# Attention scores in 64x64 products, exponentials head by head on ScalarE, and a new plan for the end of the experts

## The reference

```
chunks = x in 16 chunks of 64 tokens; Xh = rfft(chunks)          # 33 frequencies
A_low  = attention over the 4 lowest frequencies of all chunks (real and imaginary parts apart):
         16 heads of 64, 4 key/value heads, 64 positions, block-causal mask,
         p = softmax(q k^T / 8), o = p v, then the output weights
A_high = gelu(causal conv of width 7) @ weights, times a gate, plus X_high
x = layernorm(x + irfft([alpha*A_low + (1-alpha)*X_low, A_high]))
top 2 of 8 experts by distance, softmax weights;  expert: (silu(x Wg + bg) * (x W1 + b1)) W2 + b2, hidden 342
x = layernorm(x + sum of the two experts' outputs, weighted)
```

## Time and profile before

| | us |
|---|---|
| median of three runs | 608.26 |
| profiled execution | 609.42 |
| its span, first to last instruction | 607.6 |
| PE / DVE / ACT / POOL busy | 525.6 / 388.7 / 350.7 / 286.1 |
| granted TensorE clock, mean | 0.925 of full |

### The profile page before, as it was taken

How to read it: one execution, slowest core, us unless ns; L and a number is a source line. 1 busy time by engine, 2 the same in 40 slices (tenths; PEclk the granted TensorE clock), 3 DMA queues, 4 the chain that set the end, 5 groups by cost and what they waited for, 6 DMA issues and landing times.

```text
span 607.6 us, 13326 instructions
## 1 busy us (share of the span) xinstructions
PE 525.6 (87%) x3849; PEld 497.2 (82%) x3849; DVE 388.7 (64%) x1109; ACT 350.7 (58%) x738; POOL 286.1 (47%) x415
## 2 busy tenths in 40 slices
PE   3878999999999750086999999999999999999990
PEld 3767998988988530075999999999999999999990
DVE  3468899888899888991433345545464646466563
ACT  3456888887888412034555555575757565656751
POOL 0132544543544200605544444466776777563654
PEclk9979999997999955567999999999999999999995
DMA  8241055146152110111000000011111111000000
GB/s 232 61 120 55 15 149 161 43 120 161 30 131 71 35 35 2 12 13 29 19 20 20 15 20 21 20 29 33 37 38 37 33 32 37 28 29 10 32 32 35
DMA packets 48974, 31.14 MB, mean 51 GB/s; under 512 B 14251, under 2 KB 46582, under 8 KB 48918
## 3 DMA queue, kind: packets, MB, share of 16 engines
q1 hardware_dynamic: 43974, 20.87, 13.5%
q0 software_dynamic: 4224, 8.75, 5.2%
q10 hardware_dynamic: 720, 0.82, 0.5%
HBM read 21.73 MB, written 8.69 MB: 50 GB/s over the span
## 4 chain that ended last, share of the span: by engine, by line
PE 51%; POOL 3%; issue 3%; DVE 2%; DMA 1%; ACT 0%; POOLq 0%; DVEq 0%
PE ps L1434 25%; PE ps L1452 17%; PE ps L1442 8%; POOL out_dram L1401 1%; PE ps L1465 1%; DMA bias_parts<-blo 0%; POOL wo L1276 0%; DMA xs<-rows_dram,idx 0%; POOL we L1278 0%; POOL blo L1283 0%; POOL xs L1296 0%; POOL bhi L1281 0%; DVE Lc L1065 0%; POOL we L1275 0%; POOL wts L1290 0%
## 5 line engine op out<-in xcount | busy, mean ns | idle before, releaser
L1434 PE MATMUL ps<-wts,xh 128*128 x624 | 155.7, 333 | 1.0 <-issue 1.0
L1606 DVE TENSOR_TENSOR h<-ps,sg 128x684 f32<-128x684 f32 x78 | 67.9, 871 | 113.3 <-PE ps L1434 113.3
L1452 PE MATMUL ps<-w2s,hT 115*128 (+1 forms) x936 | 117.5, 275 | 1.0 <-DVE xs L1617 1.0
L1412 POOL TENSOR_TENSOR xl<-xT,xh 127x128 fp32r<-127x128 f32 x156 | 68.3, 459 | 102.1 <-ACT xh L1509 97.1
L1452 PEld LDWEIGHTS ps<-w2s,hT 115*128 115x128 f32 (+1 forms) x936 | 110.7, 191 | 1.4 <-issue 1.4
L1434 PEld LDWEIGHTS ps<-wts,xh 128*128 128x128 f32 x624 | 105.9, 192 | 1.4 <-issue 1.3
L1434 PE MATMUL ps<-wts,xl 128*128 x312 | 100.4, 322 | 0.0
L1520 ACT ACTIVATE sg<-ps 128x684 f32<-128x684 f32 x78 | 57.9, 742 | 68.6 <-PE ps L1434 68.3
L1528 ACT ACTIVATE hT<-ps 114x768 f32<-114x768 f32 x78 | 63.2, 810 | 56.9 <-PE ps L1442 56.0
L1617 DVE SCALAR_TENSOR_TENSOR xs<-ps,xs 128x128 f32 x156 | 54.3, 348 | 36.2 <-PE ps L1452 30.5
L1401 POOL DMA_INDIRECT out_dram<-xs,idx x64 | 63.0, 984 | 24.4 <-issue 18.1
(11 more groups left out here) (281 smaller groups left out, 878.9 us busy)
## 6 DMA issues: line engine op xcount, KB each, us to landing
xt<-_attn_hidden_states_dram SPq DMA_DIRECT2D x8, 512.0 KB, 6.0
xres<-_attn_hidden_states_dram SPq DMA_DIRECT2D x7, 512.0 KB, 5.3
rows_dram<-x1s SPq DMA_DIRECT2D x7, 512.0 KB, 3.7
w2s<-in_L_ffn_W_dram SPq DMA_DIRECT2D x8, 171.0 KB
st<-in_L_ffn_Wg_dram SPq DMA_DIRECT2D x8, 171.0 KB, 3.1
st<-in_L_ffn_W_dram SPq DMA_DIRECT2D x8, 171.0 KB, 3.6
stl<-in_L_ffn_Wg_dram SPq DMA_DIRECT2D x8, 171.0 KB, 3.5
stl<-in_L_ffn_W_dram SPq DMA_DIRECT2D x8, 171.0 KB, 4.1
```

The lines of the kernel that those rows point to most:

```text
L1412: v.tensor_tensor(xl[0:D - 1, i % 2, u, :], xT[0:D - 1, bass.ds(off[u], P)], xh[0:D - 1, i % 2, u, :].bitcast(F32), ALU.subtract).then_inc ...
L1434: mm = pe.matmul(ps[:, 2 * w + u, 0:HF], a[:, t % 2, u, :], wflat[:, bass.ds(w1[u] + (b + w * HF), HF)], start=(k == 0), stop=(k == 2))
L1452: mm = pe.matmul(ps[:, 6 + u, 0:D], hT[0:n, t % 2, u, k, :], w2flat[0:n, bass.ds(w1[2 + u] + k * D, D)], start=(k == 0), stop=(k == 2))
L1606: v.tensor_tensor(h[:, t % 2, :, :], ps[:, 2:4, 0:HF], sg[:, :, :], ALU.mult).then_inc(s["h_done"], 1)
```

## The change

Phase 1, scores. `QB` holds the queries without zeros, scaled by 1/8 in the eviction (two instructions a step in place of four). Each pair of heads is multiplied as two products of 64x64 weights, one with partitions 0 to 63 into PSUM partitions 0 to 63, one with 64 to 127. DVE takes only the maximum, negated. ACT takes the exponential slice by slice, straight from PSUM, with the negated maximum as bias, and writes the sum of the slice with `accum_out`. The subtraction and the sum on DVE go.

Phase 1, POOL. The three instructions for the squared norm move behind the next step's weight subtraction.

Phase 2. The last iteration runs its one real unit and writes its down product to other banks, so that it doesn't wait for the accumulation before it; the groups of tiles are smaller from tile 40 on; DVE issues up to nine pieces of normalisation an iteration, and after the last iterations 3 x 3; ACT and POOL take the iterations from a simulation of that plan (`norm_steps`).

```diff
-        QB = sb("QB", [P, 2, NHP, 2, LT])
+        QB = sb("QB", [P, 2, NHP, LT])
...
-            v.memset(QB[:, :, :, :, :], 0.0).then_inc(s["prep_cst"], 1)
...
                         for n in range(NHP):
-                            mm = pe.matmul(ps[:, 4 + i, n * LT:(n + 1) * LT], QB[:, i, n, :, :].rearrange("p a t -> p (a t)"),
-                                           kT[:, n // 2, i, :], start=False, stop=(n == NHP - 1))
+                            for h in range(2):
+                                q0 = h * HD
+                                mm = pe.matmul(ps[q0:q0 + HD, 4 + i, n * LT:(n + 1) * LT], QB[q0:q0 + HD, i, n, :],
+                                               kT[q0:q0 + HD, n // 2, i, :], start=False, stop=(n == NHP - 1))
...
-                        for h in range(2):
-                            q0 = h * HD
-                            nc.scalar.activation(QB[q0:q0 + HD, :, 4 * r:4 * r + 4, h, :]...,
-                                                 ps[q0:q0 + HD, 4 + r, :]..., ACT.Copy).then_inc(s["q_ev"], 1)
+                        nc.scalar.activation(QB[:, :, 4 * r:4 * r + 4, :].rearrange("p i n t -> p n i t"),
+                                                 ps[:, 4 + r, :]..., ACT.Copy, scale=1.0 / 8).then_inc(s["q_ev"], 1)
...
                 def softmax(i):
-                    act.wait_ge(s["sub_done"], 2 * t + i + 1)
-                    nc.scalar.activation(Sb[:, i, :, :], Sb[:, i, :, :], ACT.Exp, scale=1.0 / 8).then_inc(s["exp_done"], 1)
+                    act.wait_ge(s["max_done"], 2 * t + i + 1)
+                    if Y:
+                        act.wait_ge(s["pn_done"], 2 * t)
+                    for n in range(NHP):
+                        ins = nc.scalar.activation(Sb[:, i, n, :], ps[:, 4 + i, n * LT:(n + 1) * LT], ACT.Exp, bias=mx[:, i, n:n + 1],
+                                                   accum_out=sm[:, i, n:n + 1])
+                    ins.then_inc(s["exp_done"], 1)
...
-                    v.tensor_reduce(mx[:, i, :], sc, AX, ALU.max).then_inc(s["max_done"], 1)
-                    dve.wait_ge(s["max_done"], 2 * t + i + 1)
                     if Y:
-                        dve.wait_ge(s["pn_done"], 2 * t)
-                    v.tensor_tensor(Sb[:, i, :, :], sc, mx[:, i, :].unsqueeze(2).broadcast_to((P, NHP, LT)), ALU.subtract).then_inc(s["sub_done"], 1)
+                        dve.wait_ge(s["exp_done"], 2 * t)
+                    v.tensor_reduce(mx[:, i, :], sc, AX, ALU.max, negate=True).then_inc(s["max_done"], 1)
...
                         dve.wait_ge(s["exp_done"], 2 * t + i + 1)
-                        v.tensor_reduce(sm[:, i, :], Sb[:, i, :, :], AX, ALU.add).then_inc(s["sum_done"], 1)
-                        dve.wait_ge(s["sum_done"], 2 * t + i + 1)
                         v.reciprocal(rs[:, i, :], sm[:, i, :]).then_inc(s["rec_done"], 1)
...
             def step(t, X, Y, T):                 # POOL
                     v.tensor_tensor(st[:, 0:2 * HF], st[:, 0:2 * HF], stl[:, :], ALU.subtract).then_inc(s["wsub_done"], 1)
+                    if T:
+                        squares(t - 1)
...
-        n = 8 if k < NT - 16 else 4 if k < NT - 4 else 2
+        n = 8 if k < NT - 24 else 4 if k < NT - 4 else 2
...
+        def units(t):
+            return min(2, UNITS - 2 * t)
+        def low(t):
+            return 6 if t < ITER - 1 else 2
...
             def down(t, w1):
-                if t:
+                if 0 < t < ITER - 1:
                     pe.wait_ge(s["acc_done"], 2 * t)
-                for u in range(2):
+                for u in range(units(t)):
...
+            def norm(t, accumulated):
+                for _ in range(NORMS):
+                    if norm_due(groups, at, t, accumulated):
+                        at[:] = [at[0] + 1, 0] if piece(*at) else [at[0], at[1] + 1]
...
+def norm_due(groups, at, t, accumulated):
+    b, j = at
+    if b == len(groups):
+        return False
+    k0, n = groups[b]
+    return j >= n or t >= k0 + j + SETTLE + (2 if accumulated else 3)
...
+def norm_steps(groups):
+    out, at = [], [0, 0]
+    for t in range(ITER + 2):
+        for accumulated in (False,) * (2 * NORMS if t < ITER else 0) + (True,) * (NORMS if t < ITER else 3 * NORMS):
+            if norm_due(groups, at, t, accumulated):
+                at[1] += 1
+                if at[1] == groups[at[0]][1] + 14:
+                    out.append(t)
+                    at[:] = [at[0] + 1, 0]
+    return out + [ITER + 2] * (len(groups) - len(out))
```

More of the change, by code:

```diff
@@ L31 @@
 WE = 4 * HF
+NORMS = 3
 GATS = 4
@@ L942, in _, with squares @@
             pool.wait_ge(s["c15_done"], 1)
+            def squares(t):
+                pool.wait_ge(s["rstd_done"], t)
+                v.tensor_tensor(ya[:, :], y0[:, :], y0[:, :], ALU.mult).then_inc(s["newton"], 1)
+                v.tensor_tensor(yb[:, :], mv[:, :, 1], c128[:, :], ALU.mult).then_inc(s["newton"], 1)
+                pool.wait_ge(s["newton"], 8 * t)
+                v.tensor_tensor(sq[:, bass.ds((t - 1) * TB, TB)], ya[:, :], yb[:, :], ALU.mult).then_inc(s["sq_done"], 1)
             def step(t, X, Y, T):
@@ L1409, in _ @@
                         pool.wait_ge(s["prep"], 3)
-                    for u in range(2):
+                    for u in range(units(i)):
                         pool.wait_ge(s["xh_done"], 2 * i + u + 1)
@@ L1416, in _ @@
                 for n in range(1 if t + GAHEAD < NT else 2):
-                    if sent < NT and normed_by(groups, group_of, sent, DONE) < t:
+                    if sent < NT and out_by[group_of[sent]] + 1 < t:
                         scatter(sent)
@@ L1445, in down @@
             def down(t, w1):
-                if t:
+                if 0 < t < ITER - 1:
                     pe.wait_ge(s["acc_done"], 2 * t)
-                for u in range(2):
+                for u in range(units(t)):
                     for k in range(3):
                         n = HG + 1 if k == 0 else HG
-                        mm = pe.matmul(ps[:, 6 + u, 0:D], hT[0:n, t % 2, u, k, :],
+                        mm = pe.matmul(ps[:, low(t) + u, 0:D], hT[0:n, t % 2, u, k, :],
                                        w2flat[0:n, bass.ds(w1[2 + u] + k * D, D)], start=(k == 0), stop=(k == 2))
@@ L1507, in _ @@
                         act.wait_ge(s["a_done"], i - 1)
-                    for u in range(2):
+                    for u in range(units(i)):
                         nc.scalar.activation(xh[0:D - 1, i % 2, u, :], xT[0:D - 1, bass.ds(off[u], P)], ACT.Copy).then_inc(s["xh_done"], 1)
                 n = 0
-                while sent < NT and n < 2 and normed_by(groups, group_of, sent, DONE) <= t:
+                while t < ITER - 1 and sent < NT and n < 2 and out_by[group_of[sent]] + 2 <= t:
                     normed(sent)
@@ L1519, in _ @@
                         act.wait_ge(s["h_done"], t)
-                    nc.scalar.activation(sg[:, :, :], ps[:, 0:2, 0:HF], ACT.Silu).then_inc(s["sg_done"], 1)
+                    nc.scalar.activation(sg[:, 0:units(t), :], ps[:, 0:units(t), 0:HF], ACT.Silu).then_inc(s["sg_done"], 1)
                 if k < NT:
@@ L1527, in _ @@
                     act.wait_ge(s["b_done"], b + 1)
-                    nc.scalar.activation(hT[0:HG, b % 2, :, :, :].rearrange("p u k m -> p u (k m)"), ps[0:HG, 4:6, 0:3 * P],
+                    n = units(b)
+                    nc.scalar.activation(hT[0:HG, b % 2, 0:n, :, :].rearrange("p u k m -> p u (k m)"), ps[0:HG, 4:4 + n, 0:3 * P],
                                          ACT.Copy).then_inc(s["hT_done"], 1)
+                n = 0
+                while t >= ITER - 1 and sent < NT and n < 2 and out_by[group_of[sent]] <= t:
+                    normed(sent)
+                    sent += 1
+                    n += 1
             for k in range(sent, NT):
@@ L1588, in _ @@
             at = [0, 0]
-            def norm(t):
-                b, j = at
-                if b == len(groups):
-                    return
-                k0, n = groups[b]
-                if j < n and t < k0 + j + DONE:
-                    return
-                at[:] = [b + 1, 0] if piece(b, j) else [b, j + 1]
+            def norm(t, accumulated):
+                for _ in range(NORMS):
+                    if norm_due(groups, at, t, accumulated):
+                        at[:] = [at[0] + 1, 0] if piece(*at) else [at[0], at[1] + 1]
             for t in range(LAST + 1):
@@ L1605, in _ @@
                     dve.wait_ge(s["a_done"], t + 1)
-                    v.tensor_tensor(h[:, t % 2, :, :], ps[:, 2:4, 0:HF], sg[:, :, :], ALU.mult).then_inc(s["h_done"], 1)
+                    v.tensor_tensor(h[:, t % 2, 0:units(t), :], ps[:, 2:2 + units(t), 0:HF], sg[:, 0:units(t), :], ALU.mult).then_inc(s["h_done"], 1)
                 if c >= 0:
                     off = offsets(mybir.EngineType.DVE, c, 2, [RTOP] * 2 + [RTOP + D + E] * 2)
-                norm(t)
-                norm(t)
+                if t < ITER:
```

(21 more changed lines are left out.)

33 lines of the change are left out of this document (15 added, 18 removed).

## The result

| | before | after |
|---|---|---|
| median of four runs, us | 607.89 | 615.48 |
| range | 607.15 to 608.27 | 614.91 to 616.23 |
| profiled execution, us (its span) | 609.42 (607.6) | 616.23 (614.4) |

The changed kernel is slower by 1.3%: the ratio is 1.0127, with a 95% interval of 1.011 to 1.0145. The forecast was 624.0 us, that is +15.7; the direction came true, the size is a little under half (+7.6). The loss lies in phase 1, and there is a small gain at the end. Timed again on three chips for the experiments, the kernel before took 603.0 to 609.7 us in two groups, one up to 605.9 and one from 607.1, and its four executions here all fall in the upper group.

The account below looks back on a forecast made before the run. Phase 1 was taken as bound by PE and an equally long softmax chain through ACT and DVE, the experts by PE. Phase 1 +18.3 and end -2.6 gave +15.7 us on 608.26: 624.0 us, range 607 to 641.

Parts of the forecast that it names:

- the formula: Phase 1 steady step: transposes of Pb start at E+1.84, where E = max(121.21, 119.67+8a)+1.92+8a and a is ACT's slice time.
- a wait before L361 for DVE's residual: Sign in phase 1: PE waits there in every step from 2 on, with steps 2 to 4 us longer.
- the size of a: ACT's time for one exponential slice of 64 columns in phase 1: 0.35 us, bounds 0.22 and 0.48.
- two overlaps in each pair: ACT's slices in phase 1: 0.29 us each; the middle 0.35 was placed between this and one overlap, 0.39.
- steps 0 and 1: First steps of phase 1, slowed by ACT's exponentials: +0.5 us in step 0, +1.6 us in step 1.
- the clock: Danger in phase 1: with PE idle some 3 us a step, the granted clock may fall more often; no separate size.
- Less time gains nothing: Scores on PE, phase 1: shorter products gain nothing, as the table load ends 0.46 us after the maximum; no change taken.
- then still end before 129.03: Phase 1 steady step: despite late Vs, PE's inverse transform and routing products end inside the 2.70 us delay.
- The end: End of the experts: the last scatters come earlier, -2.6 us, bounds -1.3 and -4.
- Free sums: Rival on ACT's exponentials in phase 1: sums cost nothing, a near 0.22, -0.4 us, 607.9 us; chance 0.13.
- Doubled scores on PE: Rival in phase 1: each smaller score product takes as long as now, +10.8 us, 634.8 us; chance 0.13.
- Faster: Rival in phase 1: ACT's slices run 0.16 us each, a below 0.18, about -5.5 us, 602.7 us; chance 0.12.

Follow-up runs that it names:

- exponentials alone: Head by head exponentials with sums on ScalarE put on the kernel before, with its 128x128 scores: 616.22 against 604.09 us, ratio 1.0183.
- the changed kernel's repeat: The changed kernel timed and profiled again, nothing altered, against the kernel before: 614.73 against 604.09 us, ratio 1.0157.
- wait filled: The changed kernel plus four unused products on PE ahead of the second transposes: 613.57 us against 605.72 for the kernel before, ratio 1.0103.
- the end alone: The changed experts behind the phase 1 of the kernel before: 604.25 against 605.34 us for the kernel before, ratio 0.9982.

## Why the prediction was wrong in size

**Right: what bounds phase 1.** The reading of the earlier trace rows, that the softmax's chain through ACT and DVE is as long as PE's queue, is what the runs show: 1.7 us less of PE a step bring 0.17, and longer exponentials come out whole, by the formula to 0.07 us (exponentials alone). The sign that I gave for it, a wait before L361 for DVE's residual in every step from 2 on, holds there; in the changed kernel it stands in steps 2 and 3 only (1.01 and 1.10 us). PE's larger wait, 2.2 us for `x1T`, comes earlier, and from step 4 on PE is late by its own queue. Also right is that 64x64 products need not be slower, and, but for that 0.17 us, that less time for them gains nothing in steps 2 to 7.

**Wrong: the size of a.** The step that failed is "I take the middle, 0.35". The trace has 0.29, the value named in that sentence as two overlaps in each pair. The bounds held (0.22, 0.48), but the upper one came from a read of 0.167 us with nothing overlapped, while the read costs 0.09 us. The terms are 16 slices a step: 0.06 x 16 = 1.0 us in each of steps 2 to 7, so +10.4 in place of +16.2, and 1.0 less in steps 0 and 1 each. That is 7.7 us too much. The whole balance from the forecast's +15.7 to the span's +6.8: -7.7 for a, -3.4 for the start and the rest of step 0, +0.6 and +0.5 for the clock and what else is in steps 1 and 2 to 7, +0.2 between phase 1 and the experts, +0.8 at the end. With a = 0.29 alone the forecast's sum would be +8.0 and look right, but that is luck: the terms that follow are missing from it and partly cancel.

**Wrong: steps 0 and 1.** "Less time gains nothing" was argued for the steady step, where the table load holds exponential 0, and carried over to two steps where it does not hold. In step 0 DVE waited for the scores. From the first score product to the second reciprocal it took 8.19 us before (27.76 to 35.95), 7.64 with the exponentials alone, and 6.79 after (26.29 to 33.08), 7.14 in the changed kernel's repeat: -0.5 is what a = 0.29 gives, and a further 0.5 to 0.9 are the shorter scores, which I had set to nothing. The rest of the -2.35 and the -1.47 of the start are not shown to be the change's: from that reciprocal to the next scores it took 15.44 us before and 14.49 after, but 16.02 in the repeat, with more of PE's products at the slow clock. In step 1 the forecast of +1.6 looks near the +1.23, by luck: without a slow stretch it is 21.19, that is -0.4, made of +0.4 for the exponentials and -0.8 for the scores, and one slow stretch of 1.6 us stands on top.

**Not priced: the clock.** The forecast named the danger and gave it no term. It said that PE's inverse transform and routing products "then still end before 129.03", which holds at the full clock (exponentials alone) and not in steps 4 to 7 of the changed kernel. The slow stretches cost 0.4 us in each of steps 4 to 6 and 0.5 in step 7 (wait filled), 1.6 in step 3 (25.25 against 23.6) and 1.6 in step 1. In steps 2 to 7 that is some 3.2 us and nearly cancels in this comparison, because the kernel before had a stretch too, with PE busy throughout: 24.73 in one step, 2.9 over its usual 21.8, which the profile of the end alone doesn't have. Without the slow stretches the change costs 6 x 1.8 = 10.9 us in steps 2 to 7, and where both were timed again and the kernel before took 604.09, the whole change costs 10.6 us and not 7.6.

**The end: -1.5 to -1.8 in place of -2.6.** The last accumulation was due at 592.6 + 8.56 = 601.2 and started at 602.33; behind it the chain of statistics and Newton steps to L1606 went as forecast (602.33 to 606.46, and the scatters 1.26 apart behind it). So the term mis-sized is the time to the last accumulation. Of its 1.1 us, 0.7 are the accumulation before it, which was due at 590.4 + 8.56 = 599.0 and started at 599.65, and 0.4 are idle time of DVE in front of it, behind its own pieces (ten instructions from 599.91 to 601.89). What causes either was not tested. The sign was wrong by more: the last scatter starts 14.4 us behind the last up product and 15.0 before, 0.6 nearer and not 2 to 3. The other 0.9 us of the gain stand ahead of that product, which before is the padding unit's and is gone after.

**The rivals.** Free sums (a near 0.22): the sum has an instruction of its own, and no run has 0.22 with it; even with the sums on DVE again, a = 0.20, the kernel is no faster than before. The Trainium skill's rule that an operation with an accumulator output is two instructions ("VectorE: DVE Perf Modes", section "Two Vector instructions with no wait between them"), stated there for VectorE, holds here for ScalarE: 128 such reads stand in the trace. Doubled scores on PE: it fell, 32 products take 1.08 us for one i where 16 took 1.93. The Trainium skill ("TensorEngine Tiling (Array Packing)", section "Gotcha 1: PSUM Pressure") says that different row tiles cannot access one PSUM bank at the same time. Both halves of each pair write the same bank here, in partitions of their own, and at 0.034 us a product nothing shows them held up. Faster: wrong for the whole. The change without its exponentials is faster by about as much, but not for that rival's reason, as a is never below 0.18.

## What to carry to other kernels

An instruction of 512 columns split into eight of 64 trades its own length for eight fixed parts; it pays only on an engine whose queue is not on the chain that sets the pace, however much work it takes off a neighbour. When one engine is busy 100% of a window, follow one step in the timelines for the chain that ends just before it needs it, as shortening the busy engine then gains the difference between the two and no more. And price the first and last steps of a pipeline by themselves: a term that is hidden in the steady step can be bare there. Before a single step is explained, look whether it repeats in another execution of the same code: a slow stretch of the clock is worth 1.6 to 2.9 us here, as much as the terms that are looked for.

## What the runs showed of the hardware that was not expected

- Products of 64x64 weights with 64 columns in fp32, in pairs on the two diagonal quarters, run at 0.034 us each: 32 in 1.08 us, against 16 of 128x128 in 1.93 (0.12 each).
- The accumulator's output on ScalarE is a record of its own (0.19 to 0.34 us) that costs 0.09 us net: slices start 0.29 us apart with it, 0.20 without.
- After 2.2 us of idle PE in a step with PE otherwise busy, the next four products took 3.3 to 3.7 us and not 1.96 in steps 4 to 7 of the changed kernel, in two profiles; in steps 2 and 3 of both they took 1.96 after the same wait. After 0.5 or 1.5 us, or with the wait filled, they kept 1.96 in every step.
- The granted clock also fell to 0.50 with PE busy throughout: from 141.4 to 148.2 us in the kernel before, where PE is busy 6.80 of 6.80 us. Another profile of the same phase 1 has no such stretch.
